# In cycles with a batch job, the second max unit is issued ahead of the job instead of behind it

## The reference, cut to what matters

```
x = x + attn_a(layernorm(x))   # 16 heads of 16, ALiBi bias, causal softmax, biases
x = x + ffn(layernorm(x))      # 8 experts, top 2; touches the first 1024 of the 8192 rows
x = x + attn_b(layernorm(x))   # 16 heads of 16, rotary positions, causal softmax
x = x + ffn(layernorm(x))
...
q, k, v = x @ W (+ b)          # per head
attn = softmax(q k^T / 4 + bias or -inf above the diagonal)
out  = (attn v) @ Wo
```

## Time and profile before

| | |
|---|---|
| median of 3 runs | 4156.4 us (4152.18 to 4167.15) |
| the profiled execution's own time | 4157.57 us |
| its span, first to last instruction | 4155.8 us |
| PE busy | 3989.5 us, 96% of the span |
| DVE, ACT, POOL busy | 2997.2 us, 2798.6 us, 846.1 us |
| granted PE clock, mean over the span | 0.990 |

### The profile page before, as it was taken

How to read it: one execution, slowest core, us unless ns; L and a number is a source line. 1 busy time by engine, 2 the same in 40 slices (tenths; PEclk the granted TensorE clock), 3 DMA queues, 4 the chain that set the end, 5 groups by cost and what they waited for, 6 DMA issues and landing times.

```text
span 4155.8 us, 108094 instructions
## 1 busy us (share of the span) xinstructions
PE 3989.5 (96%) x42400; PEld 2460.7 (59%) x42401; DVE 2997.2 (72%) x4046; ACT 2798.6 (67%) x5828; POOL 846.1 (20%) x1176
## 2 busy tenths in 40 slices
PE   6999999999999999999999999999999999999998
PEld 4555555555555555557865555555555555558854
DVE  5888888887878788873038888888888878881074
ACT  2677777777777777775247777777777777773264
POOL 3100001111111123231022333333323232110020
PEclk8999999999999999999999999999999999999999
DMA  6322233324333343235553333333333333345522
GB/s 182 76 57 54 61 82 79 70 75 88 81 77 78 84 104 104 81 102 172 178 156 84 93 91 90 94 98 98 98 91 96 86 77 87 68 103 191 181 71 71
DMA packets 246892, 406.29 MB, mean 98 GB/s; under 512 B 29307, under 2 KB 161859, under 8 KB 233283
## 3 DMA queue, kind: packets, MB, share of 16 engines
q1 hardware_dynamic: 243310, 390.99, 35.8%
q0 software_dynamic: 3072, 8.39, 0.8%
HBM read 263.78 MB, written 121.21 MB: 93 GB/s over the span
## 4 chain that ended last, share of the span: by engine, by line
PE 48%; ACT 4%; DVE 3%; issue 2%; DMA 1%; SPq 0%; ACTq 0%; POOL 0%; DVEq 0%
PE ps_acc L1027 12%; PE ps_r L966 9%; PE ps_p L996 8%; PE ps_p L1137 5%; PE ps_r L1150 5%; ACT probs L848 4%; PE ps_r L1065 3%; DVE part_max L1326 2%; PE ps_r L1073 2%; PE ps_r L1069 1%; PE ps_r L971 1%; PE ps_p L990 1%; PE ps_p L1003 0%; PE ps_r L962 0%; PE ps_r L1058 0%
## 5 line engine op out<-in xcount | busy, mean ns | idle before, releaser
L1326 DVE TENSOR_REDUCE part_max<-ps_p 128x2 f32<-128x1024 f32 (+3 forms) x2560 | 2625.5, 1061 | 654.4 <-PE ps_p L996 496.4
L848 ACT ACTIVATE probs<-ps_r 128x512 f32<-128x512 f32 (+1 forms) x4608 | 2335.2, 575 | 667.0 <-PE ps_r L966 402.2
L966 PE MATMUL ps_r<-q_stack,k_stack 54*128 54x512 f32 (+3 forms) x5120 | 1381.3, 392 | 31.4 <-ACT probs L848 27.9
L996 PE MATMUL ps_p<-k_stack,q_stack 52*128 52x512 f32 (+3 forms) x5120 | 1238.2, 425 | 49.9 <-DVE part_max L1326 25.3
L1027 PE MATMUL ps_acc<-probs,v_head 128*17 128x256 f32 x19456 | 1146.1, 361 | 1.6 <-ACT probs L848 1.6
L966 PEld LDWEIGHTS ps_r<-q_stack,k_stack 54*128 54x128 f32 x5120 | 727.3, 187 | 261.7 <-ACT probs L848 212.7
L1027 PEld LDWEIGHTS ps_acc<-probs,v_head 128*17 128x17 f32 x19456 | 488.8, 97 | 463.0 <-issue 224.1
L996 PEld LDWEIGHTS ps_p<-k_stack,q_stack 52*128 52x128 f32 x5120 | 556.6, 186 | 343.3 <-issue 161.4
L1401 DVE COPY xf<-ps_r 128x256 f32<-128x256 f32 x60 | 25.5, 425 | 402.3 <-PE ps_r L1150 402.3
L911 ACT ACTIVATE hid_f<-ps_p 128x256 f32<-128x256 f32 x240 | 92.0, 383 | 301.7 <-PE ps_p L1137 301.7
L971 PE MATMUL ps_r<-id,mk 64*128 64x64 bf16 x3558 | 280.6, 194 | 0.0
(11 more groups left out here) (134 smaller groups left out, 2408.0 us busy)
## 6 DMA issues: line engine op xcount, KB each, us to landing
probs<-w_dram SPq DMA_DIRECT2D x58, 1024.0 KB, 7.1
q_stack<-parts SPq DMA_DIRECT2D x384, 128.0 KB
k_stack<-parts SPq DMA_DIRECT2D x384, 128.0 KB
parts<-pa SPq DMA_DIRECT2D x128, 256.0 KB, 2.5
parts<-pb SPq DMA_DIRECT2D x128, 256.0 KB, 3.5
o_sums<-acc_sb SPq DMA_DIRECT2D x1008, 17.0 KB
swp<-tmp SPq DMA_DIRECT2D x128, 128.0 KB
bk<-recips SPq DMA_DIRECT2D x58, 256.0 KB
```

The costliest lines, as they stand in the source:

```text
L848: act.activation(probs[:, at % PBUF, u, 0:w], block_bank(g, n, u)[:, 0:w], ACT.Exp)\
L966: mm = pe.matmul(bank[:, col:col + QW - q0], ks[s][r, kb * P:(kb + 1) * P], qs[s][r, qt * QW + q0:(qt + 1) * QW], start=fresh, stop=True, ...
L996: mm[u] = pe.matmul(banks[:, u, col:col + w], qs[s][r, qb * P:(qb + 1) * P], ks[s][r, kc * QW:kc * QW + w], start=fresh, stop=True, skip_g ...
L1326: mm = dve.tensor_reduce(part_max[:, :, qb, kc], ps_p[:, p1_banks(g, n), col:col + w], AX_X, ALU.max)
```

## The change

The second unit of a cycle that has a job is issued between score n of head 0 and the job, no longer behind the job, and its masks come behind its matmuls. Nothing else is changed, neither the work nor the order of the other engines.

```
                     if has_job(g, n):
                         unit(g + 1, n, masks_first=after_value)
                         score(g, n, 0)
+                        unit(g + 1, n + 1)
                         for j in JOBS[g][n]:
                             job(*j)
-                        unit(g + 1, n + 1, masks_first=True)
                         score(g, n, 1)
                         score(g, n + 1, 0)
                         unit(g + 1, n + 2)
```

## The result

The kernel became slower: 4180.6 us (median of 7 runs, 4170.3 to 4195.1) against 4156.4 (7 runs, 4149.0 to 4167.2). The ratio is 1.0062, with a 95% interval from 1.004 to 1.0084. The prediction was 4144, with a range up to 4167, so the time lies 36.6 us above the forecast and outside its range.

What follows compares the result with a forecast made beforehand. PE, busy 96% of the span, was taken to bound the kernel. Terms -22.0 + 2.3 + 2.5 + 4.5 = -12.7 us from 4157.6 gave 4144.9, stated as 4144 against the median; range 4126 to 4167.

Steps and rivals of the forecast that it cites:

- the tight copy: ACT's copy of a job frees the second score's bank late: 0.05 us lost per layer-a `qk`, 0.18 per `xt`.
- plain cycles: 239 cycles with one job, no masks in the second unit: 0 by order, +2.3 and +2.5 us from copies.
- The third rival: The job's copy holds the second score in every cycle: some 0.13 x 350 = 45 us, 4189; chance 0.13.
- the ring holds the second job: With 3 PSUM banks, the second of two jobs waits for an exponential to free its bank, losing 0.46 us.
- the hole: PE's 0.46 us wait ahead of the second of two jobs, which the moved unit was to fill with 0.23.
- The gain of one slot: Where two jobs stand in a cycle, one pair of matmuls fits into PE's wait: 0.23 us gained per cycle.
- Two-job cycles: 111 cycles: 90 x 0.23 = 20.7 us, less 0.8 for layer-a `qk`, plus 2.1 with `xt`: -22.0 us.
- `xt` in one-job cycles, n = 0: 14 cycles where the `xt` copy delays the second score by 0.18 us each, +2.5 us in all.
- The masked cycles: 169 cycles with masks in the second unit: about +0.04 us in n = 12 and 32, 0 in 24; +4.5 us.
- the bounds of -8 and +25: Limits for the 169 cycles with masks: all hidden, -8 us; each paying 0.15 anew, +25 us.
- The rule that weight loads of 94 and 186 ns would set the gap behind a job: Skill's load rule: if the gap followed the load, masks leaving the front would cost 15.5 us more, sum about +3.

Runs made afterwards that it cites:

- short copies: ACT copies only 64 of 256 columns of `qk`, `v`, `y` jobs from the second sequence on; ratio to before: old order 1.0007, new order 1.0017.
- the doubled masks: Masks of the second unit in n = 12, 24, 32 issued twice, in the kernel before and the changed one; 4167.9 and 4193.1 us.
- The first part of the change: Kernel before, with the unit issued ahead only in the 111 cycles with two jobs; 4136.3 us, ratio 0.9953.

## Why the prediction was wrong

**The step that failed** is the lag of the tight copy: "with the 0.05 of lag the score can start at +1.69", "copies of 0.384 end at +1.55 and hold nothing up", and hence "The two cancel: **0** for the 239 cycles". The starts of the scores came out exactly so (+1.69 and +1.63). What the step left out is that the semaphore holds the score's weight load, which in these cycles had run 0.18 to 0.23 ahead of its matmul, and that the next start, the value product's, pays for it. I had taken 0.05 from one start of a matmul behind an exponential and looked no further than the last score. The load of that very matmul stood beside it in the trace, held as well:

```profile
909.32 0.30 PEld L1065 LDWEIGHTS ps_r<-xT,wqkv 128*128 128x128 f32 x2 [0.48 <-ACT probs L848]
```

With the load it reads: product = end of copy + 0.05 + 0.43. For a copy that ends at +1.55 that is +2.03 against 1.96, so 0.07 lost; for one at +1.64 it is +2.12, so 0.16. Measured cycle by cycle, the 165 plain cycles with `v`, `y` or a layer-b `qk` lost 0.07 to 0.08, the 45 with a layer-a `qk` 0.16, the 14 with `xt` 0.24, and the 15 with `c` alone nothing. The term came to 21.2 us where 4.8 stood. The short copies show the cause: with them the product is back at 0.33.

**The third rival** named this mechanism ("the copy of the job holds the second score in every cycle") with a chance of 0.13. The sign that the prediction named for it, many waits of line 966 for lines 884, 889 and 895, appeared (66, 52 and 49), on PEld. Its place and price were off: not the score's start but its load, and not 0.13 in 350 cycles but some 0.09 on average in 239 and in those two-job cycles whose unit n+2 has no masks. The lag that was to decide it, 0.05, was right.

**Point by point.**
- That PE sets the pace, and the ring holds the second job: right. The waits fell to 6.1 us (predicted: some 12).
- The unit takes 0.23 in the hole, the second job stays at 0.9: right. The gain of one slot is right as well: with short copies the two-job cycles gave -22.7.
- Two-job cycles: -16.2 instead of -22.0. In n = 28 the slot came whole (7.02 to 6.78 with `qk`, 7.08 to 6.84 with `y`), since masks of unit n+2 cover the copy, and the product stands 0.41 behind the score in both. In n = 4 it was 0.06 for the layer-a `qk` instead of 0.18, and 0.12 to 0.14 for the others instead of 0.23, for the same held load. `xt` gave 0 in n = 4, and 0.11 in n = 28.
- `xt` in one-job cycles, n = 0: +0.24 each instead of +0.18, the held load once more. The whole slot is lost: the product follows the job by 1.77 in both orders.
- The masked cycles: +16.0 instead of +4.5, within the bounds of -8 and +25. The term was mis-sized: +0.06, +0.11 and +0.11 for n = 12, 24 and 32 instead of +0.04, 0 and +0.04. The prediction itself named over 0.1 each as a sign of being wrong, and two of the three kinds reached it. I had said that mask slots merely change places; additional ones do, as the doubled masks show, and a fixed cost remains. The step that failed here is that the unit was to get cheaper by a slot's difference in its new place, 0.23 instead of 0.34, with or without masks: with them it takes 0.44 to 0.45 in either place. Why is open. Room for free masks in the opening pair behind a job would explain it, but the first 8 masks took 0.13 there and 8 more took 0.12, so there is little sign of it.
- The rule that weight loads of 94 and 186 ns would set the gap behind a job, at 15.5 us: the gap is 709.26 to 710.33, 1.07, with a full load in front, and was 1.06 with masks in front. The trace doesn't bear the rule out here, and the 11.5 us that the masked cycles cost beyond the forecast aren't in that gap. Masks in front, in the new place, returned 3.0 us of them by the cycles. The 11.5 goes by the medians of the cycles; by the runs at equal clock it is less (11.3 - 4.5 = 6.8).

Together the errors are 5.8 + 16.4 + 11.5 + 0.3 = 34.0 us in the cycles, and the median lies 36.6 above the forecast.

## What to carry to other kernels

Where a buffer's wait stands at a matmul that brings its own weights, the tight time is that of the weight load. Here nothing was lost when the release came 0.16 us ahead of the matmul's start (0.05 of lag and 0.11 of lead). Give it that slack, and read the waits of the load queue, not those of the matmul, before calling it free. A hole in front of a held job is better closed by letting a job that isn't held go first than by moving work in from behind, since what moves away from behind the job was also the cover of the next release. And when an edit is good in one kind of cycle and bad in another, put a condition on it: here the two-job cycles alone gave 0.9953 where the whole gave 1.0062.

## What the runs showed of the hardware

- A weight load held by a semaphore until its matmul is due starts together with it (928.34), and the next step's start follows the load by 0.42 to 0.43. Where the load leads its matmul by 0.11 or more (0.18 at 916.76), the next step follows the matmul by 0.32.
- The granted clock of one execution was 0.50 from 4090 to 4130 us, while PE was busy for 38.6 of 40 us. PE was busy for 16.94 of 20 us in the window from 4050, at a clock of 0.82, and for 19.04 in the window from 4070, at 0.67. Before had a window like the first (16.31 of 20 us, 0.83) and went back to 1.00. What decides between the two stays open.
- Runs of one kernel spread with the mean granted clock, by 2.1 to 4.0 us for each 0.001. The first part of the change ran at 0.991 against 0.989, and about 5 of its 20 us are that.
- The same kernel before took 4156 us in three of the comparisons (4156.4, 4156.4, 4156.9) and 4218.4 in the one on the slower chip, at a mean granted clock of 0.981 instead of 0.989. By medians the cycles are as long there (the old order with short copies sums up to 1.6 us more than before on the first chip); a few long cycles make the difference. Absolute times set side by side would have misread the short copies by some 60 us.
